# A perceiver block: output projection and feed-forward joined in one block, feed-forward loads placed beside the self-attention, attention outputs normalised once per head

## What is computed

```python
x = x + xattn(layernorm(x), ctx)    # 16 heads of 64; the 4 x 2048 context rows are one set of 8192 keys
x = x + attn(layernorm(x))          # rotary, causal, within a batch of 128; then @ Wo + bo
x = x + ffn(layernorm(x))           # fp4 weights with a scale per group of 128
# xattn: q, k, v rounded to 127 levels, probabilities to 255 levels of the row's largest; then @ Wp + bp
# ffn:   y = (silu(x @ Wg) * (x @ Wu)) @ Wd;  y / sqrt(mean(y * y) + 1e-6)
```

## Time and profile before

| | us |
|---|---|
| median of three runs | 2915.75 |
| profiled execution, its own time | 2918.6 |
| its span (first to last instruction) | 2916.8 |
| TensorE matmul busy | 2616.7 (90%) |
| VectorE busy | 1856.0 (64%) |
| ScalarE busy | 1042.6 (36%) |
| GpSimd busy | 551.9 (19%) |
| mean granted TensorE clock | 0.963 |

### The profile page before, as it was taken

How to read it: one execution, slowest core, us unless ns; L and a number is a source line. 1 busy time by engine, 2 the same in 40 slices (tenths; PEclk the granted TensorE clock), 3 DMA queues, 4 the chain that set the end, 5 groups by cost and what they waited for, 6 DMA issues and landing times. The chain is left out here.

```text
span 2916.8 us, 42666 instructions
## 1 busy us (share of the span) xinstructions
PE 2616.7 (90%) x16824; PEld 1331.0 (46%) x16824; DVE 1856.0 (64%) x2875; ACT 1042.6 (36%) x930; POOL 551.9 (19%) x208
## 2 busy tenths in 40 slices
PE   6999999999999999999777777777769999499998
PEld 3444444444444444444344444444444476244443
DVE  5855555555555555555699999999934343466663
ACT  3111111111111111111389999999942132211100
POOL 0400000000000000000364654654510811011100
PEclk9999999999999999999899999999979977699999
DMA  6243444344434443343478888888762200300000
GB/s 239 71 102 85 109 115 105 82 108 115 102 88 105 115 108 88 99 115 100 131 174 209 183 193 211 180 197 203 159 212 87 87 1 1 61 15 15 8 1 29
DMA packets 557201, 321.44 MB, mean 110 GB/s; under 512 B 401952, under 2 KB 533280, under 8 KB 552352
## 3 DMA queue, kind: packets, MB, share of 16 engines
q1 hardware_dynamic: 557088, 319.78, 43.2%
HBM read 149.82 MB, written 69.21 MB: 75 GB/s over the span
## 5 line engine op out<-in xcount | busy, mean ns | idle before, releaser
L498 PE MATMUL kv_acc<-kv_whi,kv_xthi 128*128 128x512 f16 x2048 | 778.1, 380 | 5.7 <-DVE kv_xtlo L554 5.7
L498 PE MATMUL kv_acc<-kv_wlo,kv_xthi 128*128 128x512 f16 x2048 | 778.0, 380 | 0.0
L498 PE MATMUL kv_acc<-kv_whi,kv_xtlo 128*128 128x512 f16 x2048 | 777.9, 380 | 0.0
L950 DVE TENSOR_SCALAR_CACHE_REDUCE at_sc<-at_score 128x1024 f32<-128x1024 f32 x512 | 612.3, 1219 | 16.9 <-PE at_score L832 12.4
L1053 ACT ACTIVATE at_sc<-at_sc,at_bias,at_qs 128x4096 uint16<-128x4096 f32 x128 | 484.8, 3790 | 1.1 <-DVE at_bias L962 1.1
L541 ACT ACTIVATE kv_parts<-kv_key 128x1024 f16<-128x1024 f32 x64 | 67.6, 1057 | 863.3 <-DVE kv_key L579 863.3
L498 PEld LDWEIGHTS kv_acc<-kv_whi,kv_xthi 128*128 128x128 f16 x2048 | 200.6, 98 | 248.2 <-DVE kv_xtlo L554 6.2
L498 PEld LDWEIGHTS kv_acc<-kv_whi,kv_xtlo 128*128 128x128 f16 x2048 | 200.6, 98 | 242.4 <-issue 1.4
L498 PEld LDWEIGHTS kv_acc<-kv_wlo,kv_xthi 128*128 128x128 f16 x2048 | 200.6, 98 | 242.0 <-issue 1.1
L560 DVE SCALAR_TENSOR_TENSOR kv_key<-kv_acc,kv_bias 128x512 f32<-128x512 f32 x128 | 88.5, 691 | 339.1 <-PE kv_acc L498 339.1
L847 PE MATMUL at_turn<-ident,at_sc 128*128 128x128 f16 x2048 | 151.3, 224 | 121.7 <-DVE at_probt L968 91.3
(11 more groups left out here) (189 smaller groups left out, 3359.6 us busy)
## 6 DMA issues: line engine op xcount, KB each, us to landing
kv_rows<-in_ctx SPq DMA_DIRECT2D x64, 512.0 KB, 8.1
keys_turned<-kv_kt SPq DMA_DIRECT2D x32, 1024.0 KB, 5.2
values<-kv_val SPq DMA_DIRECT2D x32, 1024.0 KB, 9.4
at_v_raw<-values SPq DMA_DIRECT2D x16, 2048.0 KB, 8.6
at_kt<-keys_turned SPq DMA_DIRECT2D x32, 512.0 KB, 5.2
x<-keys_turned SPq DMA_DIRECT2D x31, 512.0 KB, 5.1
wq_stage<-in_wkv SPq DMA_DIRECT2D x4, 2048.0 KB, 7.8
x<-in_x SPq DMA_DIRECT2D x2, 2048.0 KB, 8.3
```

Of the source, the lines that this page charges most:

```text
L498: last = nc.tensor.matmul(acc[c][:], a[s][:, k, :], b[:, c, k, :], start=(k == 0 and q == 0), stop=(k == KD - 1 and q == 2))
L950: nc.vector.tensor_scalar(sc[n % 2][:, c * SC:(c + 1) * SC], score[pos % 2][:], 1.0, None, ALU.mult, ALU.max, accum_out=part_max[n % 2][:, ...
```

## The change

- In the cross-attention the four slots of a head write their products side by side into one bank. `total_sum`, `inverse` and `output` are made once per head: the first two in the head's next slot (chunks 5 and 6), the output in the slot after (chunk 0), over 128 x 256. The value scale is no longer applied there; GpSimd multiplies by it in `move_out`, and waits for the move of the head before last ahead of fetching that scale.
- The output bias is not loaded at the start of `pp`; SyncE loads it in the second block of `attend_causal`, with the first three word loads and all scales.
- Panel 9 (second half of the output weights) is split in `attend_causal`: high part on ScalarE after group 4, low part on VectorE before group 8.
- `po` and `feed_forward` become one block, `project_and_feed_forward`. For each tile both halves of the output projection are made, then VectorE takes them, normalises that tile and TensorE turns it behind the next tile's products. Chunk 0 of the weights is made before the first take, chunk 1 behind the last tile's low parts, ahead of the first hidden values. Both scalings of the scales are made behind the turns of the attention's output.
- Rooms are shared by hand in one tensor `space` and in the panels' buffers, in place of tensors with lives of their own. The sizes of tiles, and the sums, are as before.

The core of the diff:

```diff
+        part_sum = [chip.sb(ctx, f"at_psum{j}", [P, T, 2], F32) for j in range(2)]
+        total = [chip.sb(ctx, f"at_total{j}", [P, T], F32) for j in range(2)]
+        inv = [chip.sb(ctx, f"at_inv{j}", [P, T], F32) for j in range(2)]
...
                 pool.wait_ge(scales_ready, 2)
+                pool.wait_ge(o_moved, MOVED0 + head + 1 - 2)
...
             def move_out(i, j):
                 head = 2 * i + j
-                pool.wait_ge(o_taken, TAKEN0 + i * SLOTS + T * (j + 1))
-                nc.gpsimd.tensor_copy(o[:, :, bass.ds(head * HD, HD)], o_pair[j][:]).then_inc(o_moved, 1)
+                pool.wait_ge(o_taken, TAKEN0 + head + 1)
+                nc.gpsimd.tensor_tensor(o[:, :, bass.ds(head * HD, HD)], o_pair[j][:],
+                                        vs_pair[j][:].unsqueeze(1).to_broadcast((P, T, HD)), ALU.mult).then_inc(o_moved, 1)
...
             def dma_sums(i, g, n, half):
                 if half == 0:
                     if n % T == 0:
-                        pe.wait_ge(v_quantised, 2 * i + n // T + 1)
-                    pe.wait_ge(o_taken, TAKEN0 + g + 1 - 2)
+                        head = 2 * i + n // T
+                        pe.wait_ge(v_quantised, head + 1)
+                        pe.wait_ge(o_taken, TAKEN0 + head + 1 - 2)
                     pe.wait_ge(dma_turned[n % 2], DMA0 + 16 * (i * (SLOTS // 2) + n // 2 + 1))
                 for b in range(half * 2 * GB, (half + 1) * 2 * GB):
-                    last = nc.tensor.matmul(outp[n % 2][:, 0:HD], probt_dma[n % 2][:, b, :], v_int[n // T][:, b, :],
+                    last = nc.tensor.matmul(outp[n // T][:, n % T, :], probt_dma[n % 2][:, b, :], v_int[n // T][:, b, :],
                                             start=(b == 0), stop=(b == 4 * GB - 1))
                 if half == 1:
                     last.then_inc(dma_summed, 1)
...
+            def total_sum(head, j):
+                dve.wait_ge(exp_done, EXP0 + 2 * T * (head + 1))
+                nc.vector.tensor_reduce(total[j][:], part_sum[j][:], AX.X, ALU.add).then_inc(inv_step, 1)
+
+            def inverse(head, j):
+                dve.wait_ge(inv_step, INV0 + 2 * head + 1)
+                nc.vector.reciprocal(inv[j][:], total[j][:]).then_inc(inv_step, 1)
+
+            def output(head, j):
+                dve.wait_ge(inv_step, INV0 + 2 * head + 2)
+                dve.wait_ge(dma_summed, DSUM0 + T * (head + 1))
+                dve.wait_ge(o_moved, MOVED0 + head + 1 - 2)
+                nc.vector.tensor_tensor(o_pair[j][:], outp[j], inv[j][:].unsqueeze(2).to_broadcast((P, T, HD)),
+                                        ALU.mult).then_inc(o_taken, 1)
...
-                        if c == 0 and not (first and n < 2):
-                            output(i if n >= 2 else i - 1, g - 2, (n - 2) % SLOTS)
-                        if c == 1 and before:
-                            turned_out(g - 1)
-                        if c == 5:
-                            biased = not (last and ahead >= SLOTS)
-                            if biased:
-                                find_max(i * SLOTS + ahead, ahead)
-                            if before:
-                                total_sum(g - 1, (n - 1) % SLOTS)
-                            if biased:
-                                make_bias(i * SLOTS + ahead, ahead)
-                        if c == 6 and before:
-                            inverse(g - 1, (n - 1) % SLOTS)
+
+                        if c == 1 and not (first and n == 0):
+                            turned_out(i * SLOTS + n - 1)
+                        done = None if n % T > 1 or first and n < 2 else 2 * i - 1 + n // T
+                        j = (n // T + 1) % 2
+                        if done is not None and n % T == 0 and c == 5:
+                            total_sum(done, j)
+                        if done is not None and n % T == 0 and c == 6:
+                            inverse(done, j)
+                        if done is not None and n % T == 1 and c == 0:
+                            output(done, j)
+                        if c == 5 and not (last and ahead >= SLOTS):
+                            find_max(i * SLOTS + ahead, ahead)
+                            make_bias(i * SLOTS + ahead, ahead)
...
+            def exps(i, g, n, e):
+                j, t = n // T, n % T
                 if e == 0:
                     act.wait_ge(bias_ready, g + 1)
-                    act.wait_ge(inv_step, INV0 + 2 * (g - 2) + 1)
-
-                j, t = n // T, n % T
+                    if t == 0:
+                        act.wait_ge(inv_step, INV0 + 2 * (2 * i + j - 2) + 1)
                 nc.scalar.activation(prob[n % 2][e], sc[n % 2][:, e * EC:(e + 1) * EC], ACT.Exp, bias=bias[n % 2][:],
-                                     scale=qs_pair[j][:, t:t + 1], accum_out=part_sum[n % 2][:, e:e + 1])\
+                                     scale=qs_pair[j][:, t:t + 1], accum_out=part_sum[j][:, t, e:e + 1])\
                     .then_inc(exp_done, 1)
...
+
+        @block.sync
+        def _(sp):
+            sp.dma_start(*row).then_inc(feed.row_loaded, 16)
+            feed.load(sp, 0)
+            feed.load_scales(sp)
+            feed.load(sp, 1)
+            feed.load(sp, 2)
...
             masks(0)
             for g in range(G):
+                if g == G // 2:
+                    panels.low(dve, split)
                 if g + 1 < G:
                     masks(g + 1)
...
                 if g + 1 < G:
                     exps(g + 1)
                 turned_out(g)
+                if g == G // 4:
+                    panels.high(act, split)
...
+class FeedLoads:
+
+
+    LOADS = [(0, 1), (1, 4), (4, 8), (8, 12), (12, 16), (16, 18)]
...
+        o_hi, o_lo = pair0
+        (w_hi0, w_lo0), (w_hi1, w_lo1) = panels.parts[first], panels.parts[first + 1]
+        h_hi, h_lo = (pair1[0], w_hi0, w_lo0), (pair1[1], w_hi1, w_lo1)
...
+            def turn_o(n):
+                t, h = units[n]
+                if n >= 4:
+                    pe.wait_ge(o_lo_ready, n - 3)
+                for k in range(4):
+                    last = nc.tensor.transpose(dn_acc[n % 4][:, k * P:(k + 1) * P], natural(o, t, 4 * h + k), ident32[:])
+                last.then_inc(o_turned, 1)
+
+            def products(t, n):
+                pe.wait_ge(o_lo_ready, 2 * t + 2)
+                if t >= 2:
+                    pe.wait_ge(wo_taken, 2 * (t - 2) + n + 1)
+                w_hi, w_lo = panels.parts[first + n]
+                tok = slice(t * P, (t + 1) * P)
+                for k in range(KD):
+                    for q, (a, b) in enumerate(((o_hi, w_hi), (o_hi, w_lo), (o_lo, w_hi))):
+                        last = nc.tensor.matmul(acc[t % 2][n][:], a[:, k, tok], b[:, k, :],
+                                                start=(k == 0 and q == 0), stop=(k == KD - 1 and q == 2))
+                last.then_inc(wo_summed, 1)
+
+            def turn_x(n):
+                t, h = units[n]
+                if h == 0:
+                    pe.wait_ge(rows_ready, t + 1)
+                if n < 4:
+                    pe.wait_ge(o_lo_ready, n + 5)
+                else:
+                    pe.wait_ge(x_lo_ready, n - 3)
+                for k in range(4):
+                    last = nc.tensor.transpose(dn_acc[n % 4][:, k * P:(k + 1) * P], by_nibble(o, t, 4 * h + k), ident32[:])
+                last.then_inc(x_turned, 1)
+
+            for n in range(len(units)):
+                turn_o(n)
+            pe.wait_ge(panels.lo_ready, first + 2)
+            for t in range(T):
+                for n in range(2):
+                    products(t, n)
+                if t:
+                    turn_x(2 * t - 2)
+                    turn_x(2 * t - 1)
+            turn_x(2 * T - 2)
+            turn_x(2 * T - 1)
+            pe.wait_ge(x_lo_ready, 2 * T)
+            pe.wait_ge(wo_taken, 2 * T)
...
             def make(c):
                 if c in (0, 1):
                     dve.wait_ge(scaled, c + 1)
+                freed = summed
+                if c == 0:
                     count = None
+                elif c == 1:
+                    freed, count = wo_summed, 2 * T
+                weights.make(dve, c, feed.words_of(c), freed, count)
```

VectorE's and ScalarE's new streams in the joined block, in short (`high_o`, `low_o`, `high_x`, `low_x` split a turned half tile):

```diff
+            def take_x(t, n):
+                cols = slice(n * HALF, (n + 1) * HALF)
+                dve.wait_ge(wo_summed, 2 * t + n + 1)
+                nc.vector.scalar_tensor_tensor(out=x[:, t, cols], in0=acc[t % 2][n][:], scalar=UNSCALE,
+                                               in1=x[:, t, cols], op0=ALU.mult, op1=ALU.add).then_inc(wo_taken, 1)
...
+            def normalise(t):
+                for n in range(2):
+                    dve.wait_ge(wo_taken, 2 * t + n + 1)
+                    nc.vector.bn_stats(stats[:, t, n, :], x[:, t, n * HALF:(n + 1) * HALF]).then_inc(stat_step, 1)
+                dve.wait_ge(stat_step, 2 * t + 2)
+                nc.vector.bn_aggr(aggr[:, t, :], stats[:, t, :, :]).then_inc(aggr_step, 1)
...
```

(63 more changed lines are left out.)

203 lines of the change are left out of this document (103 added, 100 removed).

## The result

The kernel after takes 2879.95 us (median of 4 runs, 2879.67 to 2880.95), the kernel before beside it 2915.32 us (4 runs): ratio 0.9875, 95% interval 0.9863 to 0.9888, so 35.4 us or 1.25% less. The forecast was 2866.6 us with a range of 2854 to 2882. Direction and range hold; the time is 13.3 us above the forecast, and above the forecast's own range of 2859 to 2874. Most of the miss is one term, the cross-attention.

A forecast was written before the change was run, and what follows sets the result against it. VectorE and ScalarE were taken to bound the cross-attention, TensorE the up products. Terms -14.3+0.3-0.5+2.8-37.5 = -49.2 us took the profiled 2918.6 to 2869.4, less 2.85 for the median: 2866.6 us, range 2854 to 2882.

The forecast's parts named there:

- Part 1: Cross-attention, normalised headwise: three small VectorE instructions per slot become three per head, -14.3 us.
- a period still at 10.8: Cross-attention: listed sign that the prediction is wrong; it expected 42.2 us per head.
- VectorE is full: Cross-attention: VectorE taken as fully busy in the slot's period of 10.80 us.
- A second way of counting: Cross-attention: the loop through the exponential, shortened in three slots of four, also gives about 1.0 us a head.
- the cross-attention gives nothing: Rival, chance 0.12: the head's output comes as one lump and lighter slots can't run ahead; 2880.9 us.
- The reading that the copy behind a reciprocal starts 0.08 after it: Cross-attention, VectorE: a removed reciprocal lasting 0.16 saves only 0.08 us a slot.
- The start of the projections: Part 2: one bias load less ahead of the first turns of the projections, -0.5 us.
- The split: Part 3, self-attention: splitting the second half of the output weights adds 1.0 on ScalarE and 1.8 on VectorE, +2.8 us.
- The early loads: Part 4: words and scales issued beside the self-attention are covered by the whole stage, cost 0.
- The joined block: Part 5, output projection to feed-forward: first up product at 2494.8 in place of 2532.27, -37.5 us.
- The stretch of low clock at the start of the up products: Feed-forward: a start at 1.2 GHz costing 2.8 us over full clock was left in, difference 0.
- the step from profiled time to median: Whole kernel: the median taken as 2.85 us below the profiled execution, carried from the kernel before.

The follow-up runs named there:

- before_turn3_first: The kernel before, with the turns of k=3 moved ahead of the first half of the value products in TensorE's order: 2899.2 us, ratio 0.994.
- after_both_orders: The kernel after, with turns of k=1 behind the scores of their step and turns of k=3 ahead of the value products: 2854.8 us, ratio 0.9789.
- the pieces: The kernel after, with the split inside the self-attention cut into four pieces on each engine, one in each of four groups: 2878.2 us, ratio 0.9872.
- after_loads_late: The kernel after, with words and scales issued at the start of the joined block, not beside the self-attention: 2895.8 us, ratio 0.9933.
- after_turn3_first: The kernel after, with the turns of k=3 moved ahead of the first half of the value products in TensorE's order: 2862.7 us, ratio 0.9814.

## Why the prediction was right in direction and 13 us too low

**Part 1 was the step that failed.** It said that the output "delays the next copy to 1814.87, so 0.30 us a slot". The times are right, the cause is not: the copy would have started at 1814.87 without the output too. It takes the scores that TensorE computes behind sixteen turns, which wait for the exponential. The loop is: end of the exponential half, turns of k=0 and 1, scores, VectorE's copy and its transposed block, turns of k=2, scores, value products, scores, turns of k=3, ScalarE's copy, exponential half. From the exponential's end to the transposed block on VectorE it is 2.74 us in both kernels: 1802.48 to 1805.22 before, 1909.98 to 1912.72 after. The prediction did name the loop, and said that it is shortened in the slots without an output. It did not walk the loop with TensorE's program order in it. Its own sign of being wrong, "a period still at 10.8", is what came. "VectorE is full" was read off rows without printed idle time; before_turn3_first shows 10.64 of work in 10.80. A second way of counting that came to the same -14.3 was no check, since both counted the output's 0.30 as VectorE's time. Its size was off too: with the loop out of the way the headwise form takes 0.60 us a head from VectorE (4 by 10.64 against 3 by 10.39 and 10.79), where 0.96 was said.

The rival "the cross-attention gives nothing" had 0.12 and gave 2880.9. It is what happened, for a reason close to its own: the head's output does come as a lump, but it costs 0.03 in its slot, and the light slots cannot run ahead. The range of 2854 to 2882 holds only because it was made to take in this rival, and the clock's 1.4 us, which nobody forecast, helped to keep the time in it.

The reading that the copy behind a reciprocal starts 0.08 after it, for a duration of 0.16, held. The Trainium skill (VectorE: DVE Perf Modes, section The DRAIN you can't avoid) has an instruction wait until the pipe is empty, though an unheld one starts earlier. The runs agree with the second: 0.20 from the start of an output of 0.28 to the next copy (before_turn3_first), 0.34 from a headwise output of 0.42 (after_both_orders).

**The start of the projections** came out as said, -0.5, with two sizes in it: from SyncE's first issue to the turns it is 4.57 us in place of 5.40, and GpSimd's last move ahead of that takes 0.72 in place of 0.40. Behind it the projections took 1.4 us less, a term that no step had.

**The split** cost 0.8 and 1.5 where 1.0 and 1.8 were said. The group stretched as the prediction walked it; with the pieces the cost is gone, so it was the length of the single instruction against the gap, not the work.

**The early loads** cost nothing visible, as said. The self-attention's windows go from DMA share 0.00 to 0.31, and its groups keep 4.72. after_loads_late, which has no early loads of words and scales, takes the same 89.34 us from the first key copy to the turns of the output.

**The joined block** was within 0.7 us: first up product at 2494.14, forecast 2494.8. TensorE's idle between tiles is nil, eight turns between products take 0.89 (the last eight, in the tail, 1.99), and the tail from the last product is 7.9 as summed from small rows. The stretch of low clock at the start of the up products stayed as assumed: 251.51 against 251.10.

The sum of the terms misses the profiled execution by 11.6 us; by the rounded rows of the table 13.4 for part 1, less 1.4 in the projections, 0.3 in the self-attention and 0.6 for the block, plus 0.4 in the feed-forward. The other 1.8 us is the step from profiled time to median, 2.85 carried over from the kernel before and 1.0 in the kernel after.

## What to carry to other kernels

An engine without printed idle time in a steady period is not proved to be the limit: ask of each instruction that follows the one to be removed when its own input was ready, and whose program order decides that. Where two or three engines hand work round in a loop, first shorten the loop by reordering the engine that has slack (here TensorE, 76% busy), then take work from the fullest one; taken alone, the second step measured as nothing here. Work put into the gaps of a tight loop should be cut to the size of the gap.

## What was unexpected of the hardware

A shorter loop cost clock. In a stage where TensorE had run at 1.00 for 550 us, one reordering brought dips to 1.2 GHz for about 3.4 us in every second head, each worth 1.1 to 1.4 us, and a second reordering, at the same mean period of the other slots, removed them. The Trainium skill (TensorE: Matmul & The Clock Gate, section What's actually happening) says that activity releases the throttle. The runs agree in direction, since both the dips and the slow turns of after_loads_late come behind waits of TensorE, 1.47 and 10.58 us. But the length of the wait does not decide it. In after_turn3_first itself the other head has the same 1.47 us ahead of its turns at 1750.78, with TensorE busy for 0.53 of the 2 us from 1749, and stays at 1.00. The kernel after waits 1.45 in this place in most slots (1913.46 above) and after_both_orders 1.47 once a head, both at 1.00. What makes one head fall and the other not is left open.
